# First-level steps of a row of LSTM levels are placed between the steps of the second level's chains (Trainium2, one core)

## The chip, the cores and the metric

The kernel runs on one core of one Trainium2 chip. The metric is the device time in microseconds (us). Before the change it was 3021.64 us, the median of 3 runs (3020.8 to 3025.89).

## What is computed

Four graph layers follow one another, each behind a layer norm and a ReLU and with a residual sum; x is 8 batches x 2048 nodes x 128 features in float32. The change touches the end of the third layer only. It applies LSTMs over windows of nodes, for p = 1 to 4, each level on the result of the one before:

```
for p in range(1, MAX_SKIP + 1):
    nw = Tv // p
    wins = h[:, :nw * p, :].reshape(Bv * nw, p, Hd)
    last = _lstm_last(Wih[p - 1], Whh[p - 1], bih[p - 1], bhh[p - 1], wins)
    idx = jnp.arange(nw) * p + (p - 1)
    h = h.at[:, idx, :].set(last.reshape(Bv, nw, Hd))
```

One step of an LSTM is `g = x_t @ Wih.T + h @ Whh.T + bias`, four gates i, f, g, o from it, `c = sigmoid(f) * c + sigmoid(i) * tanh(g)` and `h = sigmoid(o) * tanh(c)`, from zero states. Level 1 is a window of one node, so it changes every node by itself. Level 2 is a chain of two steps (nodes 2m and 2m+1) and replaces the second node, level 3 a chain of three steps, level 4 one of four.

## The kernel before

The program is a row of stages; the recurrence, function `recurrences` (L1861), comes before the last graph product and the perceptron. It handles two batches (k = 0, 1) at once, a pair, and four pairs one after another. The features lie on the 128 partitions and the 2048 nodes on the columns, sorted by their residue modulo 4, so that each residue is a block of 512 columns.

**The steps.** `lstm_units` (L1829) lists 18 steps: 0 to 3 are level 1, one for each residue; 4 and 5 a chain of level 2 (residues 0 and 1), 6 and 7 the other (residues 2 and 3); 8 to 10 and 11 to 13 the two chains of level 3; 14 to 17 the chain of level 4. A `Unit` has its level p, its place q in the chain, its columns, and `source`, the last earlier step whose result it reads as input. A step with q = 0 has no hidden part and no forget gate: 3 gates. The others have 4 gates and two parts. Every engine walks through this list, for each step k = 0 and then k = 1.

**TensorE**, `gates_of` (L2215): float32 values are split into a high and a low part, so a gate is 3 matmuls (L2239, or L2244 for columns in descending pieces) for the input part and 3 more (L2253) for the hidden part. Before the input part it waits for the low part of its source (`low`) and for the gates of the step before to have been read out of PSUM (`activated`, L2234), since each batch has one set of four banks. Before the hidden part it waits for the low part of the step before (L2250).

**ScalarE**, `evaluate` (L2049): one activation for each gate (L2058). The first waits until the cell update of the step before is done, the output gate until the output of the step before is done, since the gate tile is single. `squash` (L2064) is the tanh of the cell (L2067).

**VectorE**: `update` (L2132) computes the cell: one operation (L2139) for q = 0, three (L2144, L2146, L2148) otherwise. The cell tile has two halves, half 0 for the cell and half 1 for the product of input gate and candidate. `output` (L2150) is three operations (L2163, L2164, L2168): high part, value and low part of h. In the last step of a chain they go to the `hx` tiles, otherwise to the small `st` tiles, which hold one state per batch.

**The order within a step**, `turns` (L1949): if `free(n)` (q = 0, and the source older than step n - 1), the cell activation and the output of each batch are put off behind the next batch's first gates. In the other steps they stand right behind their own update:

```
yield 0, ((n - 1, 1) if n and free(n) else None), free(n)
yield 1, ((n, 0) if free(n) else None), n + 1 < NU and free(n + 1)
```

**Work beside it.** The layer norm of the pair before is woven in: on VectorE its statistics in eight parts behind steps 0 to 7 (`MEASURE`, L1925, L146), with an aggregation behind 3 and 7; POOL then takes a power (L170); on ScalarE the normalisation in parts behind steps 5 to 8 and 12 to 15 (`NORMALISE`, L182). ScalarE splits the next pair's input behind steps 9 and 16 (`SPLIT`), and POOL subtracts for its low part (L2017). In the first pair the weights of levels 2 to 4 are split ahead of steps 1, 2 and 3 (`BEHIND`, L2129). SP's queue loads and stores whole batches, and its order does not depend on the list.

## Time and profile before

| | us |
|---|---|
| median of 3 runs | 3021.64 |
| profiled execution | 3023.62 |
| its span, first to last instruction | 3021.8 |
| TensorE busy with matmuls | 2755.8 (91%) |
| VectorE busy | 1660.1 (55%) |
| ScalarE busy | 1325.6 (44%) |
| POOL busy | 172.3 (6%) |

A row of a timeline gives the start from the start of the span, the duration, the engine, the line of the kernel and the tiles; several instructions alike may be merged (x3). In brackets stands the idle time of that engine before it and what released it; where an instruction waits for several semaphores, the one that came last by the profile is named. A matmul starts before the one before it has drained, so the distance of two starts is what it takes of TensorE. PE is TensorE, DVE VectorE, ACT ScalarE, POOL GpSimd.

### The profile page before, as it was taken

Reading aid. Unit: us, or ns where it says so; the run is one execution under the profiler, and the core shown is the slowest. Engines: PE = TensorE matmul, PEld = TensorE weight load, DVE = VectorE, ACT = ScalarE, POOL = GpSimd, SP = SyncE. Lnnn points to the kernel's source line nnn. Section 1 sums busy time; section 2 is a strip of 40 time slices with the busy share of each in tenths; the row PEclk is TensorE's granted clock in tenths of the full one; section 3 lists DMA queues with packets and bytes.
Section 4 is the critical chain, followed back from the end, with each engine's and each line's share of the span. In section 5 each row is a group of like instructions: output and inputs, shape, how many; then the busy total and the mean of one; then the engine's idle time right before and its main releaser. Section 6 shows DMA issues by size and latency. Waiting matters only on the chain. (4 is left out here: it accounts for less than half of the span.)

```text
span 3021.8 us, 38552 instructions
## 1 busy us (share of the span) xinstructions
PE 2755.8 (91%) x14565; PEld 2325.4 (77%) x14565; DVE 1660.1 (55%) x3206; ACT 1325.6 (44%) x2161; POOL 172.3 (6%) x98
## 2 busy tenths in 40 slices
PE   7799998899999969999999997898989869999977
PEld 7578887899999958888877875777777757778743
DVE  7766764677777643213322124888887864332246
ACT  2765554566666532112211113666767763221135
POOL 2000102000001000000000000001010000000000
PEclk9999997999999979999999999999999989999998
DMA  8544544322223153124321223111212135331258
GB/s 349 185 150 165 179 164 149 97 61 85 71 70 98 43 177 112 56 64 145 113 70 57 66 67 108 43 43 29 84 28 56 28 84 194 98 94 56 77 205 297
DMA packets 241840, 325.88 MB, mean 108 GB/s; under 512 B 13792, under 2 KB 155136, under 8 KB 237440
## 3 DMA queue, kind: packets, MB, share of 16 engines
q1 hardware_dynamic: 238208, 310.99, 31.8%
q10 hardware_dynamic: 3456, 12.58, 1.0%
q8 instruction: 105, 1.72, 0.2%
q14 instruction: 71, 0.58, 0.1%
HBM read 226.91 MB, written 96.62 MB: 107 GB/s over the span
## 5 line engine op out<-in xcount | busy, mean ns | idle before, releaser
L993 PE MATMUL l_acc<-l_a_hi,l_g_hi 128*128 128x512 f32 x1536 | 602.6, 392 | 35.1 <-DVE l_g_lo L921 29.0
L993 PE MATMUL l_acc<-l_a_lo,l_g_hi 128*128 128x512 f32 x1536 | 599.4, 390 | 0.0
L993 PE MATMUL l_acc<-l_a_hi,l_g_lo 128*128 128x512 f32 x1536 | 599.2, 390 | 0.0
L913 DVE TENSOR_TENSOR l_a_lo<-l_raw,l_a_hi 128x512 fp32r<-128x512 f32 x192 | 132.7, 691 | 754.1 <-ACT l_a_hi L863 754.1
L1449 PE MATMUL n_acc<-n_hb,n_p 128*128 128x129 f32 x4096 | 472.3, 276 | 25.1 <-DVE n_p L1365 19.9
L863 ACT ACTIVATE l_a_hi<-l_raw 128x512 fp32r<-128x512 f32 x192 | 121.1, 631 | 846.5 <-PE l_acc L993 818.2
L1449 PEld LDWEIGHTS n_acc<-n_hb,n_p 128*128 128x128 f32 x4096 | 464.3, 192 | 29.2 <-issue 15.6
L993 PEld LDWEIGHTS l_acc<-l_a_hi,l_g_hi 128*128 128x128 f32 x1536 | 289.5, 188 | 97.0 <-DVE l_g_lo L921 29.2
L1365 DVE SCALAR_TENSOR_TENSOR n_p<-n_e,n_cols,c_mT 128x2048 f32<-128x2048 f32 x128 | 296.7, 2345 | 89.7 <-ACT n_e L1326 71.0
L2058 ACT ACTIVATE r_gate<-r_ps,r_bias 128x512 f32<-128x512 f32 (+2 forms) x504 | 298.0, 639 | 103.4 <-PE r_ps L2253 77.8
L993 PEld LDWEIGHTS l_acc<-l_a_lo,l_g_hi 128*128 128x128 f32 x1536 | 289.5, 188 | 61.3 <-issue 1.4
L993 PEld LDWEIGHTS l_acc<-l_a_hi,l_g_lo 128*128 128x128 f32 x1536 | 289.4, 188 | 60.4
L1326 ACT ACTIVATE n_e<-n_row,n_cols 128x2048 f32<-128x2048 f32 x128 | 261.7, 2088 | 13.4 <-DVE n_p L1365 11.0
L676 PE MATMUL l_acc<-l_a_hi,l_g_hi 128*128 128x512 f32 x512 | 201.1, 393 | 22.3 <-DVE l_a_lo L581 18.5
L676 PE MATMUL l_acc<-l_a_lo,l_g_hi 128*128 128x512 f32 x512 | 199.9, 390 | 0.0
L676 PE MATMUL l_acc<-l_a_hi,l_g_lo 128*128 128x512 f32 x512 | 199.9, 390 | 0.0
L2239 PE MATMUL r_ps<-r_hx_hi,r_w_hi 128*128 128x512 f32 (+2 forms) x376 | 141.8, 377 | 18.2 <-ACT r_gate L2058 13.5
L2239 PE MATMUL r_ps<-r_hx_lo,r_w_hi 128*128 128x512 f32 (+2 forms) x376 | 139.1, 370 | 0.0
L2239 PE MATMUL r_ps<-r_hx_hi,r_w_lo 128*128 128x512 f32 (+2 forms) x376 | 138.9, 369 | 0.0
L2253 PE MATMUL r_ps<-r_st_hi,r_w_hi 128*128 128x512 f32 (+2 forms) x288 | 110.1, 382 | 25.4 <-DVE r_st_lo L2168 25.4
L676 PEld LDWEIGHTS l_acc<-l_a_hi,l_g_hi 128*128 128x128 f32 x512 | 96.6, 189 | 45.5 <-DVE l_g_lo L597 18.2
L460 ACT ACTIVATE l_raw<-l_raw 128x512 f32<-128x512 f32 x128 | 79.5, 622 | 94.2 <-DMA l_raw<-in_adjT_dram 94.0
(263 smaller groups left out, 3797.0 us busy)
## 6 DMA issues: line engine op xcount, KB each, us to landing
l_raw<-in_adjT_dram SPq DMA_DIRECT2D x256, 256.0 KB, 2.8
l_raw<-in_rows_dram SPq DMA_DIRECT2D x64, 256.0 KB, 3.0
l_hraw<-h SPq DMA_DIRECT2D x32, 512.0 KB, 3.4
z<-l_res SPq DMA_DIRECT2D x64, 256.0 KB, 2.7
m_z<-z SPq DMA_DIRECT2D x16, 1024.0 KB, 5.2
l_xt<-in_x_dram SPq DMA_DIRECT2D x30, 512.0 KB, 3.5
d_xt<-in_x_dram SPq DMA_DIRECT2D x16, 512.0 KB, 15.6
n_hb<-h SPq DMA_DIRECT2D x8, 1024.0 KB, 5.9
```

Of the source, the lines that this page charges most:

```text
L460: last = act.activation(raw[:, gp % R, k], raw[:, gp % R, k], ACT.Copy, accum_out=parts[:, k, gp % T, gp // T:gp // T + 1])
L676: last = pe.matmul(acc[:, b], lhs[:, s, b * D:(b + 1) * D], rhs[:, gp % R], start=(s == 0 and lhs is g_hi and rhs is a_hi), stop=(s == T - ...
L863: act.activation(a_hi[:, gp % RING], raw[:, gp % RING], ACT.Copy).then_inc(a_high, 1)
L913: dve.tensor_tensor(a_lo[:, gp % RING], raw[:, gp % RING], a_hi[:, gp % RING].bitcast(F32), ALU.subtract).then_inc(a_low, 1)
L993: last = pe.matmul(acc[:, b], lhs[:, s, b * D:(b + 1) * D], rhs[:, gp % RING], start=(s == 0 and lhs is g_hi and rhs is a_hi), stop=(s == ...
L1326: act.activation(e[:, j % DEPTH], row[:, b.par], ACT.Relu, bias=cols[:, b.par, 1, j:j + 1], scale=cols[:, b.par, 2, j:j + 1]).then_inc(rai ...
L1365: dve.scalar_tensor_tensor(pr[:, j % DEPTH].rearrange("p (c i) -> p c i", i=P), e[:, j % DEPTH].rearrange("p (c i) -> p c i", i=P), cols[: ...
L1449: last = pe.matmul(acc[:, k, o:o + D + 1], pr[:, j % DEPTH, t * P:(t + 1) * P], hb[:, b.par, j], start=(j == 0 and o == 0), stop=(j == T - 1),
L2058: act.activation(gate[k][:, g, 0:size], ps[k][:, g, 0:size], ACT.Tanh if g == 2 else ACT.Sigmoid, bias=bias[:, 2, units[n].p - 1, g:g + 1] ...
L2239: last = pe.matmul(halves_of(ps[k][:, g, 0:size], unit, unit.length), wg, runs_of(h[k], unit.runs, unit.length), start=(m == 0), stop=(q = ...
L2253: last = pe.matmul(ps[k][:, g, 0:size], w[:, 1, p - 1, g * D:(g + 1) * D], h[k][:, 0:size], start=False, stop=(m == 2), skip_group_check=n ...
```

## The change

The list of steps is put in another order: level 1 of residues 0 and 1, first step of the first chain of level 2, level 1 of residue 2, second step of the first chain, level 1 of residue 3, then both steps of the second chain (6 and 7). Levels 3 and 4 keep their places. The sources follow the new numbers. A level 1 step now holds its cell in half 1 of the cell tile (`cell_of`), because the cell of a chain stays in half 0 across it. `chained` gives the step whose hidden state a step reads, `raw_step` the number of a level 1 step among its like, and `RAW_READ` the step from which the pair's input tiles are free for POOL's next subtraction.

```diff
--- before.py
+++ after.py
@@ -1829,12 +1829,13 @@
 def lstm_units():
 
     block = lambda s: RESIDUE_AT[s] * 512
-    units = [Unit(1, 0, 512, [block(s)], 512, 512, -1) for s in range(SKIP)]
-    for first in (0, 2):
-        for q in range(2):
-            units.append(Unit(2, q, 512, [block(first + q)], 512, 512, first + q))
+    first_level = lambda s: Unit(1, 0, 512, [block(s)], 512, 512, -1)
+    second = lambda first, q, source: Unit(2, q, 512, [block(first + q)], 512, 512, source)
+
+    units = [first_level(0), first_level(1), second(0, 0, 0), first_level(2), second(0, 1, 1), first_level(3),
+             second(2, 0, 3), second(2, 1, 5)]
     piece = lambda m: block(m % SKIP) + THIRD_AT[m // SKIP]
-    for g, length, kept, sources in ((2, 170, 170, (5, 7, 7)), (0, 172, 171, (7, 5, 5))):
+    for g, length, kept, sources in ((2, 170, 170, (4, 7, 7)), (0, 172, 171, (7, 4, 4))):
         for q in range(3):
             units.append(Unit(3, q, 2 * length, [piece(3 * g + q), piece(3 * g + 3 + q)], length, kept,
                               sources[q]))
@@ -1918,6 +1919,7 @@
         block = ctx.enter_context(nc.Block())
         NPAIR = B // 2
         NRAW = sum(u.p == 1 for u in units)
+        RAW_READ = max(n for n, u in enumerate(units) if u.p == 1) + 1
         SPLIT = {NRAW + 5: 0, NRAW + 12: 1}
         NL = NU - 1
 
@@ -1941,6 +1943,17 @@
         def later(i):
 
             return not isinstance(i, int) or i > 0
+
+        def cell_of(k, n):
+
+            return cell[k][:, 1 if units[n].p == 1 else 0, 0:units[n].size]
+
+        def chained(n):
+
+            return max(m for m in range(n) if units[m].p == units[n].p)
+
+        def raw_step(n):
+            return sum(u.p == 1 for u in units[:n])
 
         def free(n):
 
@@ -2012,7 +2025,7 @@
             def split_next(i):
 
                 for k in pair:
-                    pool.wait_ge(summed[k], i * NG + before[NRAW])
+                    pool.wait_ge(summed[k], i * NG + before[RAW_READ])
                     pool.wait_ge(raw_high[k], i + 2)
                     pool.tensor_tensor(raw_lo[k][:, :], raw[k][:, :], raw_hi[k][:, :].bitcast(F32),
                                        ALU.subtract).then_inc(raw_split[k], 1)
@@ -2064,7 +2077,7 @@
             def squash(i, n, k):
                 size = units[n].size
                 act.wait_ge(cell_ready[k], i * NU + n + 1)
-                act.activation(tc[k][:, 0:size], cell[k][:, 0, 0:size], ACT.Tanh).then_inc(squashed[k], 1)
+                act.activation(tc[k][:, 0:size], cell_of(k, n), ACT.Tanh).then_inc(squashed[k], 1)
 
             def normalise(i, k, blocks):
                 b = i * 2 + k
@@ -2131,7 +2144,7 @@
 
             def update(i, n, k):
                 size, q = units[n].size, units[n].q
-                c, ig = cell[k][:, 0, 0:size], cell[k][:, 1, 0:size]
+                c, ig = cell_of(k, n), cell[k][:, 1, 0:size]
                 ga = lambda g: gate[k][:, g, 0:size]
                 at = i * NG + before[n]
                 dve.wait_ge(activated[k], at + 2)
@@ -2218,9 +2231,9 @@
                 first = isinstance(i, int) and i == 0
                 if first and (n == 0 or p > units[n - 1].p):
                     pe.wait_ge(w_split, 2 * p - 1)
-                if first and n < SKIP - 1:
-                    pe.wait_ge(first_split[k], n + 1)
-                elif n == (SKIP - 1 if first else 0):
+                if p == 1 and first and raw_step(n) < SKIP - 1:
+                    pe.wait_ge(first_split[k], raw_step(n) + 1)
+                elif p == 1 and raw_step(n) == (SKIP - 1 if first else 0):
                     pe.wait_ge(raw_split[k], i + 1)
                 elif p > 1:
                     pe.wait_ge(low[k], i * NL + unit.source + 1)
@@ -2247,7 +2260,7 @@
                     if q == 0:
                         last.then_inc(summed[k], 1)
                 if q:
-                    pe.wait_ge(low[k], i * NL + n)
+                    pe.wait_ge(low[k], i * NL + chained(n) + 1)
                     for g in gates[n]:
                         for m, (w, h) in enumerate(h_parts):
                             last = pe.matmul(ps[k][:, g, 0:size], w[:, 1, p - 1, g * D:(g + 1) * D],
```

## Rows read from the trace of the kernel before

**Rows 1.** The page, its first line
```profile
span 3021.8 us, 38552 instructions
```

**Rows 2.** Busy time by engine (instructions), clock, DMA: steps 0 to 7, second pair
```profile
core 0: us, PE busy (x) PEld busy (x) DVE busy (x) ACT busy (x) POOL busy (x), PEclk, DMA share, GB/s
2014.40:2073.90 59.50, 51.02 (x204) 38.85 (x205) 51.78 (x116) 43.59 (x74) 3.74 (x2) 0.97 0.13 36
```

**Rows 3.** TensorE's waits in the recurrence: us in total, times, longest
```profile
PE r_ps L2253 <- DVE r_st_lo L2168: 25.4, 17, 4.5
PE r_ps L2239 <- ACT r_gate L2058: 19.2, 20, 3.3
```

**Rows 4.** TensorE's timeline, second pair: start, us, instruction, [idle before]
```profile
2033.03 0.50 PE L2239 MATMUL r_ps<-r_hx_hi,r_w_hi 128*128 128x512 f32 x1 [0.24 <-ACT r_gate L2058]
...
2036.49 0.47 PE L2239 MATMUL r_ps<-r_hx_hi,r_w_hi 128*128 128x512 f32 x1 [1.10 <-DVE r_hx_lo L2168]
...
2039.01 0.50 PE L2239 MATMUL r_ps<-r_hx_hi,r_w_hi 128*128 128x512 f32 x1 [0.17 <-ACT r_gate L2058]
...
2046.60 0.79 PE L2253 MATMUL r_ps<-r_st_hi,r_w_hi 128*128 128x512 f32 x1 [4.54 <-DVE r_st_lo L2168]
...
2050.84 0.40 PE L2239 MATMUL r_ps<-r_hx_hi,r_w_hi 128*128 128x512 f32 x1
...
2061.22 0.50 PE L2239 MATMUL r_ps<-r_hx_hi,r_w_hi 128*128 128x512 f32 x1 [0.42 <-ACT r_gate L2058]
...
2065.46 0.50 PE L2253 MATMUL r_ps<-r_st_hi,r_w_hi 128*128 128x512 f32 x1 [1.17 <-DVE r_st_lo L2168]
...
2073.96 0.32 PE L2239 MATMUL r_ps<-r_hx_hi,r_w_hi 128*128 128x340 f32 x1
```

**Rows 5.** Busy time by engine and granted clock in three stretches
```profile
1888.30:1899.20 10.90, 7.70 (x30) 5.39 (x30) 10.48 (x18) 7.72 (x13) 0.00 (x0) 1.00 0.72 192
2033.00:2041.90 8.90, 7.60 (x30) 5.40 (x30) 8.61 (x38) 5.97 (x10) 0.51 (x1) 1.00 0.01 2
2046.60:2050.90 4.30, 4.30 (x13) 3.46 (x14) 3.24 (x8) 1.93 (x3) 0.00 (x0) 0.65 0.00 0
```

**Rows 6.** VectorE's timeline, second pair, from the end of slot 2
```profile
2032.96 0.87 DVE L146 BATCH_NORM_STATS2 rln_six<-r_xt 128x6 f32<-128x128 f32 x4
...
2033.75 0.68 DVE L2139 TENSOR_TENSOR r_cell<-r_gate 128x512 f32<-128x512 f32 x1
...
2036.34 0.68 DVE L2139 TENSOR_TENSOR r_cell<-r_gate 128x512 f32<-128x512 f32 x1
...
2041.22 0.69 DVE L2139 TENSOR_TENSOR r_cell<-r_gate 128x512 f32<-128x512 f32 x1
...
2041.82 0.71 DVE L2163 TENSOR_TENSOR r_hx_hi<-r_gate,r_tc 128x512 fp32r<-128x512 f32 x1
...
2050.29 0.69 DVE L2144 TENSOR_TENSOR r_cell<-r_gate 128x512 f32<-128x512 f32 x1 [0.96 <-ACT r_gate L2058]
...
2053.25 0.69 DVE L2163 TENSOR_TENSOR r_hx_hi<-r_gate,r_tc 128x512 fp32r<-128x512 f32 x1 [0.77 <-ACT r_tc L2067]
```

**Rows 7.** ScalarE's timeline, second pair
```profile
2035.66 1.85 ACT L2058 ACTIVATE r_gate<-r_ps,r_bias 128x512 f32<-128x512 f32 x3 [0.57 <-DVE r_hx L2164]
...
2041.94 0.63 ACT L2067 ACTIVATE r_tc<-r_cell 128x512 f32<-128x512 f32 x1 [1.83 <-DVE r_cell L2139]
...
2057.29 1.64 ACT L182 ACTIVATE r_hn<-r_xt,rln_shift,rln_scale 128x128 f32<-128x128 f32 x4
```

**Rows 8.** TensorE's timeline: step 5's hidden part, first pair
```profile
1899.23 0.67 PE L2253 MATMUL r_ps<-r_st_hi,r_w_hi 128*128 128x512 f32 x1 [2.16 <-DVE r_st_lo L2168]
```

**Rows 9.** POOL's timeline, second pair
```profile
2041.39 3.28 POOL L170 TENSOR_TENSOR rln_scale<-rln_var_eps,rln_half 128x16 f32<-128x16 f32 x1 [36.35 <-DVE rln_var_eps L159]
...
2094.82 4.62 POOL L2017 TENSOR_TENSOR r_raw_lo<-r_raw,r_raw_hi 128x2048 fp32r<-128x2048 f32 x1 [8.47 <-ACT r_raw_hi L2086]
```

**Rows 10.** VectorE's timeline at POOL's subtraction
```profile
2095.57 4.23 DVE L2144 TENSOR_TENSOR r_cell<-r_gate 128x340 f32<-128x340 f32 x1 [1.04 <-ACT r_gate L2058]
```

## The prediction

> **What bounds the kernel now.** I read the page first, then the stretches of the recurrence, then TensorE's waits there, then each engine's timeline through one pair of batches. (n,k) is step n of the unit list for batch k of the pair; a light step has 3 gates and no hidden part, a heavy one 4 gates and both parts.
>
> The span is 3021.8 us [rows 1]; the diff touches only the recurrence. In a pair's first eight steps (the four of level 1 and the four of level 2) VectorE is busy 51.8 of 59.5 us, as much as TensorE's 51.0 [rows 2]. TensorE waits 25.4 us for VectorE's low part of a hidden state and 19.2 us for ScalarE's gates over all pairs [rows 3]. The largest single wait is in step 5: its input part starts at 2039.01 and is 12 matmuls long, then the hidden part starts only at 2046.60, 4.54 us late [rows 4]. Two more follow, 0.42 at (6,0) and 1.17 at (7,0). After the 4.54 us the granted clock of that stretch is 0.65, so part of it ran at 1.2 GHz and not 2.4 [rows 5].
>
> Why 4.54: five light steps stand in a row. From 2065.46 to 2073.96 TensorE runs 36 matmuls (the hidden part of one batch, 12, and the whole step of the other, 24) [rows 4]: 0.235 us each, so 2.8 us for a part of a heavy step, 5.6 for a heavy step of one batch, 2.1 for a light one and 4.2 for a light one of both batches. VectorE needs for a light step 2 x (0.6 update + 2.0 output), as from 2033.75 to 2036.34, and 0.8 of layer-norm statistics (2032.96 to 2033.75), 6.0 us [rows 6]. So it falls behind by 1.8 us a step, and the fourth statistics part with its aggregation costs 2.3 (2033.75 to 2041.22 is 7.47, less 5.2) [rows 6]. Step 5 needs the state of step 4, the newest thing VectorE has.
>
> **The change, part by part.**
>
> *Instructions.* None is added or removed; the same matmuls, activations, vector operations and DMAs are issued. No DMA is moved: SP's order is the same. POOL's split waits for step 5's sums instead of step 3's, and then, as now, for ScalarE's copy that follows step 9; cost nothing, covered by those four steps. The other half of the cell tile costs nothing: same shape, same engines. Weight splits stay behind steps 0 to 2, and level 2's are finished before (2,0); nothing.
>
> *Removed.* The chain 0-1 of level 2 becomes steps 2 and 4 with a light step between. (4,0) starts its input part at 2033.03 as step 4 does now (same gate condition), ends it 2.8 us later at 2035.9, and needs the state of (2,0), which VectorE finishes before its slot 3 begins at 2033.75 [rows 6]. So the 4.54 goes, and the slow clock behind it: 12 matmuls took 4.24 us (2046.60 to 2050.84) [rows 4] and not 2.80, 1.44 us.
>
> *What is late next.* I carry the second pair's clock times on. Step 3 now ends with the output of (3,1), which is put off today, so VectorE's slot 3 is 2.0 longer, and with 2.3 of statistics ends at 2043.2. The update of (4,0), 2.0 us for a heavy one (its activation can follow at 2052.5, as 2053.25 less 0.77 tells) [rows 6], ends at 2045.3. ScalarE's cell activation of (4,0) must wait for it (0.63 us, as the one at 2041.94) [rows 7], and because step 4 is heavy it is not put off: the four gates of (4,1) stand behind it on ScalarE. They have been summed since 2044.5 but are read from 2045.9 to 2048.3 (0.58 apart) [rows 7]. TensorE runs (4,0) and (4,1) through to 2044.3, (5,0) to 2046.4, and (5,1) must wait for these gates until 2048.4: a new wait of 1.7 us. VectorE then has the output of (4,0) to 2048.1, the update of (4,1) to 2050.1, 0.78 of statistics; ScalarE's last gate of (5,0) comes at 2051.5, that of (5,1) at 2053.7. So (6,0) waits 0.8 and starts 2051.5, (6,1) 0.2 and starts 2053.8. A normalisation part of 1.6 us (the four at 2057.29) [rows 7] and the output of (5,0) put the last gate of (6,0) at 2057.5: (7,0) waits 1.5. Its input part ends at 2060.4, and the state of (6,0), third in VectorE's row behind the output of (5,1) and the update of (6,1), is there at 2062.2: 1.7 more. From 2062.3 TensorE has 2.8 + 5.6 us without a wait: step 8 starts at 2070.7. Today it starts at 2073.96 [rows 4]. **Gain 3.3 us a pair.** Check by waits: today 4.54 + 0.42 + 1.17, 1.10 at (4,1), 0.2 at (5,0), and 1.44 of clock, 8.9 together; after, 1.7 + 0.8 + 0.2 + 1.5 + 1.7 = 5.9. That gives 3.0, near enough.
>
> The first pair has no statistics, but weight splits in their place; its wait in step 5 is 2.16 [rows 8] with matmuls of 0.67 us behind it, and by the same steps its gain comes out at 3.5. I take 3.3 x 4 = 13.2 us. From step 8 on the order is the old one, and both VectorE (its heavy update of step 7 ends at 2072.4 and now at about 2075.5) and TensorE enter it about 3.3 earlier, so the gain is kept.
>
> *The clock.* New waits of 1.5 to 1.7 are not shown today. The wait of 1.10 at 2036.49 [rows 4] left the clock at 1.00; the 2.16 of the first pair [rows 8], behind 10.9 us with TensorE busy 7.70 [rows 5], did not. A fall at (7,0) would reach the end whole, 1.44 a pair; bounds 0 and 1.44, and twice that if (5,1) falls too. 1.6 lies midway between the two observed cases, so I charge half of 1.44, 2.9 us in all. 13.2 - 2.9 = **10.3 us saved**.
>
> The profiled execution took 3023.62 (its span and 1.8 around it), so the sum gives 3013.3 for it. The median of the runs shown is 3021.64, 2.0 lower; from that, **3011.3 us**.
>
> **POOL beside the heavy update.** The power operation of the layer norm starts as the statistics end, 3.28 us long at 2041.39; now it would start at 2043.3, beside the heavy update of (4,0). Beside it today VectorE's operations with two SBUF inputs kept 0.69 to 0.71 [rows 6]. But beside POOL's 4.62 us subtraction at 2094.82 [rows 9] VectorE's heavy update operation took 4.23 us for 340 columns, where 512 take 0.69 [rows 10]. I charge 0, since the same short POOL operation stands beside the same kind of vector operation; the bound is 3.3 a pair.
> By the Trainium skill (SBUF — State Buffer, two separate sides) a vector operation with two SBUF inputs and a POOL operation that reads SBUF share one port pair by an exclusive lock held for the whole instruction, and the loser blocks. The trace agrees for the long subtraction and not for the 128x16 power. Taken at its word the rule would block the update for 3.28 us, in three pairs; it is the slower rival below.
>
> **Rivals.**
> *The clock gives it back.* It falls both at (5,1) and at (7,0) in every pair: 4 x 2 x 1.44 = 11.5 of 13.2, saving 1.7: **3020**. For it: the waits come closer together, and 2.16 was enough once. Against: at (5,1) ScalarE and VectorE, not TensorE, set the pace, so most of that fall is hidden. 0.17.
> *POOL stops the heavy update (slower).* If the power blocks VectorE for 3.3 us at (4,0), all that I derived behind 2043 moves by 3.3 in three pairs, 9.9 us; the wait at (5,1) becomes 5.0, more than today's 4.54, so the clock surely falls there and probably at (7,0): 4 x 2 x 1.44 = 11.5. 13.2 - 9.9 - 11.5 = 8.2 slower: **3030**. It decides from 3.3 us of delay a pair. Against it: the 0.69 to 0.71 beside the power now. 0.08.
> *More than my table.* The clock never falls and the input-side gaps close: at most VectorE's idle time in the stretch, 59.5 - 51.8 = 7.7 a pair [rows 2], of which the start and each heavy step's wait for its own activation (0.77 before 2053.25) [rows 6] stay. I put it at 5.0 a pair: **3001.6**. 0.07.
> *The forecast*, 7 to 17 us saved: 0.66. The rest, 0.02, is left over.
>
> **The numbers.** Range: below 3003 lies most of the last rival, above 3021 the slower one and a piece of the clock's. A measurement of this kernel can tell about 0.2%, 6 us. Faster by more than 6: the forecast, the last rival, nothing of the others: 0.73. Within: the clock's rival and a sliver: 0.18. Slower: 0.09.
>
> **What would show it.** TensorE's wait for the low state falls from 25.4 to about 13 us (the first chain's gone, 2.16 in the first pair [rows 8] and 4.54 in the second, with the other two taken like it 15.8 in all; the second chain's grown by 0.5 to 1.2 a pair), and its wait for gates grows from 19.2 to about 30, with a new 1.7 at (5,1). From the first matmul of a pair to step 8: 56.2 us instead of 59.5. The update of (4,0) keeps 0.69 a piece beside POOL's power. The granted clock stays above 0.8 in any 4 us of the stretch in about half of the pairs. I am wrong if a wait of over 4 us stands at (5,1) or (7,0), if VectorE's heavy update beside the power takes 3 us, or if step 8 comes less than 1.5 us or more than 5 us earlier.

## The result, and the profile after

The changed kernel took 3010.09 us (median of 7 runs, 3005.25 to 3017.99), the kernel before it 3022.22 on the same chip (7 runs, 3020.8 to 3029.3): ratio 0.9956, 95% interval 0.9946 to 0.9967. 3011.3 had been forecast. The profiled execution took 3011.66 us, 1.8 of it around its span; the profiled one of before took 3023.62, so the two traces that are compared here lie 11.96 us apart.

The page's first line, beside [rows 1] (the number of instructions is the same):

```profile
span 3009.9 us, 38552 instructions
```

Busy time by engine, granted clock and DMA of the changed kernel. The first row is the recurrence, from the first matmul of the first pair to the start of the last row of transposes (shown below), the second row all that follows, the third and fourth are steps 0 to 7 of the second and the third pair (columns as in [rows 2]):

```profile
1863.20:2453.40 590.20, 529.44 (x2584) 442.58 (x2584) 482.57 (x935) 419.41 (x764) 49.23 (x18) 0.98 0.18 51
2453.40:3009.90 556.50, 487.36 (x1937) 353.30 (x1937) 214.26 (x371) 163.54 (x231) 7.87 (x7) 0.95 0.45 146
...
2012.30:2068.40 56.10, 49.70 (x204) 37.84 (x205) 51.31 (x116) 42.52 (x74) 3.93 (x2) 1.00 0.14 38
2161.30:2217.50 56.20, 50.05 (x206) 38.10 (x205) 51.32 (x115) 42.70 (x74) 3.79 (x2) 0.99 0.13 38
```

The same two stretches of before:

```profile
1862.60:2467.40 604.80, 537.75 (x2585) 448.33 (x2585) 484.14 (x935) 423.43 (x763) 49.13 (x18) 0.96 0.17 50
2467.40:3021.80 554.40, 488.02 (x1937) 354.93 (x1937) 214.19 (x371) 163.34 (x231) 7.88 (x7) 0.95 0.44 147
```

The last row of transposes in the changed kernel, where its first stretch ends:

```profile
2453.43 1.94 PE L2281 MATMUL r_ps<-k_ident,r_hx 128*128 128x128 f32 x16 [1.33 <-DVE r_hx L2177]
```

The recurrence is 14.6 us shorter (604.80 less 590.20), more than the whole span gained. What follows it, which the change does not touch, took about 2 us more, and the recurrence began 0.6 later. TensorE's busy time in the recurrence is 8.3 us less for the same matmuls, and its granted clock 0.98 instead of 0.96: its idle time there falls by 6.3 (from 67.1 to 60.8). So nearly half of the gain is waits and the rest is clock. For the second pair [rows 2] has 59.50 us at 0.97, the row above 56.10 at 1.00.

The time of each stage, taken as the difference of two starts in TensorE's timeline (first matmul of a pair, first of step 8, first row of transposes behind step 17):

| pair | steps 0 to 7, before | after | saved | steps 8 to 17, before | after |
|---|---|---|---|---|---|
| first | 62.91 | 59.54 | 3.37 | 83.06 | 83.66 |
| second | 59.47 | 56.05 | 3.42 | 88.17 | 85.92 |
| third | 59.36 | 56.17 | 3.19 | 88.04 | 87.82 |
| fourth | 59.57 | 55.88 | 3.69 | 80.32 | 80.34 |

13.67 us are saved in steps 0 to 7, much the same in each pair, and none is given back in steps 8 to 17. These 13.67 are what the change brings. The other 0.9 of the recurrence's 14.6 is the clock at places that the change does not touch: in steps 8 to 17 of the second pair it fell before and not after (2.25 saved), and at the turn from the second to the third pair it fell after and not before (0.9 lost).

TensorE's waits in the recurrence, beside [rows 3] (us in total, times, longest):

```profile
PE r_ps L2252 <- ACT r_gate L2071: 28.9, 24, 3.2
PE r_ps L2266 <- DVE r_st_lo L2181: 13.7, 12, 1.8
```

TensorE's timeline, second pair, beside [rows 4]; the last row is the first pair's hidden part of (7,0), the longest such wait there, where [rows 8] had 2.16 in step 5:

```profile
2033.81 0.39 PE L2266 MATMUL r_ps<-r_st_hi,r_w_hi 128*128 128x512 f32 x1
...
2046.15 0.50 PE L2252 MATMUL r_ps<-r_raw_hi,r_w_hi 128*128 128x512 f32 x1 [1.69 <-ACT r_gate L2071]
...
2049.21 0.50 PE L2252 MATMUL r_ps<-r_hx_hi,r_w_hi 128*128 128x512 f32 x1 [0.70 <-ACT r_gate L2071]
...
2055.23 0.50 PE L2252 MATMUL r_ps<-r_hx_hi,r_w_hi 128*128 128x512 f32 x1 [1.34 <-ACT r_gate L2071]
...
2059.92 0.50 PE L2266 MATMUL r_ps<-r_st_hi,r_w_hi 128*128 128x512 f32 x1 [1.63 <-DVE r_st_lo L2181]
...
2068.42 0.32 PE L2252 MATMUL r_ps<-r_hx_hi,r_w_hi 128*128 128x340 f32 x1
...
1914.23 0.50 PE L2266 MATMUL r_ps<-r_st_hi,r_w_hi 128*128 128x512 f32 x1 [1.80 <-DVE r_st_lo L2181]
```

The hidden part of (4,0) starts at 2033.81 behind its input part with no bracket: the 4.54 us are gone. In their place stand 1.69 at (5,1), 0.70 at (6,0), 1.34 at (7,0) and 1.63 at its hidden part.

VectorE's timeline at the heavy update of (4,0):

```profile
2038.21 0.69 DVE L2181 TENSOR_TENSOR r_hx_lo<-r_hx,r_hx_hi 128x512 fp32r<-128x512 f32 x1
2038.82 0.87 DVE L146 BATCH_NORM_STATS2 rln_six<-r_xt 128x6 f32<-128x128 f32 x4
...
2041.09 0.68 DVE L2157 TENSOR_TENSOR r_cell<-r_gate 128x512 f32<-128x512 f32 x1
2041.69 0.71 DVE L2159 TENSOR_TENSOR r_cell<-r_gate,r_cell 128x512 f32<-128x512 f32 x1
2042.43 0.69 DVE L2161 TENSOR_TENSOR r_cell<-r_cell 128x512 f32<-128x512 f32 x1
```

ScalarE's, behind it:

```profile
2043.16 0.63 ACT L2080 ACTIVATE r_tc<-r_cell 128x512 f32<-128x512 f32 x1 [5.28 <-DVE r_cell L2161]
2043.70 3.56 ACT L2071 ACTIVATE r_gate<-r_ps,r_bias 128x512 f32<-128x512 f32 x6
```

POOL's, in the same time:

```profile
2041.26 3.27 POOL L170 TENSOR_TENSOR rln_scale<-rln_var_eps,rln_half 128x16 f32<-128x16 f32 x1 [38.36 <-DVE rln_var_eps L159]
```

ScalarE stands 5.28 us for the cell of (4,0) and only then reads the sums of (4,1), as the forecast had it. POOL's power overlaps all three operations of the heavy update (the first for most of its length), and they keep 0.68 to 0.71 us.

### The profile page after: what moved, and what is told of

It is laid out like the page before. It is cut to its first block and busy times, and to the rows that moved or that the text cites. A ratio compares the mean times of both kernels' runs of the same rounds, so it can differ in the third digit from the quotient of the medians.

```text
span 3009.9 us, 38552 instructions
## 1 busy us (share of the span) xinstructions
PE 2746.2 (91%) x14565; PEld 2318.1 (77%) x14565; DVE 1658.9 (55%) x3206; ACT 1321.1 (44%) x2161; POOL 172.3 (6%) x98
## 5 line engine op out<-in xcount | busy, mean ns | idle before, releaser
L2080 ACT ACTIVATE r_tc<-r_cell 128x512 f32<-128x512 f32 (+2 forms) x144 | 84.9, 590 | 91.0 <-DVE r_cell L2161 81.6
```

What stands on the lines that cost most here:

```text
L2080: act.activation(tc[k][:, 0:size], cell_of(k, n), ACT.Tanh).then_inc(squashed[k], 1)
```

## The experiments

Each was timed in five rounds beside the kernel before. Since what follows the recurrence scatters (below), the recurrence itself is given too: the first matmul of the first pair to the start of the last row of transposes, in the one profiled execution; before 604.8, after 590.2.

**1. Is it the separation of the two steps, or the number of light steps ahead?** The chain of level 2 earlier, but its two steps side by side:

```diff
-    units = [first_level(0), first_level(1), second(0, 0, 0), first_level(2), second(0, 1, 1), first_level(3),
-             second(2, 0, 3), second(2, 1, 5)]
+    units = [first_level(0), first_level(1), second(0, 0, 0), second(0, 1, 1), first_level(2), first_level(3),
+             second(2, 0, 4), second(2, 1, 5)]
```

> The changed kernel with another order of the list: level 1 of residues 0 and 1, then both steps of the first chain side by side, then level 1 of residues 2 and 3, then the second chain. No step stands between the steps of a chain, but only three light steps stand ahead of the first heavy one. Theory 1 (VectorE's backlog: it needs 6.0 us for a light step where TensorE needs 4.2, so what counts is how many light steps stand in a row ahead of a heavy one): the wait of the first chain's hidden part falls from 4.5 to about 2.5 us in pairs 2 to 4, the first eight steps take about 56.9 us (before 59.5, changed 56.1), 8 to 11 us saved against before; up to 1.4 a pair less if the clock falls. Rival (distance: what counts is a step between producer and reader): the 4.5 us wait stays, within 3 us of before.

Measured: 3021.14 us (12 runs), before 3024.81 (20 runs), ratio 0.9986 (0.9975 to 0.9997); recurrence 600.8. TensorE's timeline, second pair:

```profile
2034.70 0.50 PE L2266 MATMUL r_ps<-r_st_hi,r_w_hi 128*128 128x512 f32 x1 [2.71 <-DVE r_st_lo L2181]
...
2065.91 0.50 PE L2266 MATMUL r_ps<-r_st_hi,r_w_hi 128*128 128x512 f32 x1 [1.81 <-DVE r_st_lo L2181]
```

Only three light steps stand ahead of the chain's second step here, where before there were five, and its hidden part waits 2.71 us, near what theory 1 had; the clock fell behind it and behind the 1.81. The third pair, where it fell once less, took 58.16 us for steps 0 to 7, the second 59.87. So the time did not follow: 3.7 us saved and not 8 to 11. Most of the gain needs the light step between the two. (The sum that run 4 leads to gives 3.1 us for this wait, with an ordinary part of the statistics, 0.8 us, in the gap and not the fourth one with its 2.3.)

**2. The light step between them, with one more light step ahead:**

```diff
-    units = [first_level(0), first_level(1), second(0, 0, 0), first_level(2), second(0, 1, 1), first_level(3),
-             second(2, 0, 3), second(2, 1, 5)]
+    units = [first_level(0), first_level(1), first_level(2), second(0, 0, 0), first_level(3), second(0, 1, 1),
+             second(2, 0, 2), second(2, 1, 4)]
```

(and the sources of level 3 follow: 5 where 4 stood.)

> The changed kernel with the list: level 1 of residues 0, 1 and 2, first step of the first chain, level 1 of residue 3, second step of the first chain, then the second chain. Five light steps stand in a row as before, but one of them between the two steps of the chain. Theory 1 in its plain form (only the number of light steps ahead counts) would leave the hidden part of the first chain late. Theory 2 (both: the backlog makes the newest state late, the distance decides whether the reader needs the newest): no wait at the first chain's hidden part, a wait of about 2 us for gates at the first batch after it, and VectorE's queue paces the rest, so the first eight steps take the same 56 to 57 us as the changed kernel, within 3 us of it in all.

Measured: 3012.30 us (6 runs), ratio 0.9962 (0.9946 to 0.9977); recurrence 590.8. No wait stands ahead of the first chain's hidden part; the two longest in the second pair, with a fall of the clock behind the first:

```profile
2051.31 0.47 PE L2252 MATMUL r_ps<-r_hx_hi,r_w_hi 128*128 128x512 f32 x1 [1.82 <-ACT r_gate L2071]
...
2059.36 0.50 PE L2266 MATMUL r_ps<-r_st_hi,r_w_hi 128*128 128x512 f32 x1 [1.21 <-DVE r_st_lo L2181]
```

Here five light steps in a row stand ahead of the chain's second step, as before, and the whole gain is there. So one step of distance inside the chain is enough, whatever the number of light steps ahead.

**3. The wait that took its place at (5,1).** The changed kernel, with the output of a chain's second step put off again wherever its forerunner is not the step just before:

```diff
-            return units[n].q == 0 and units[n].source < n - 1
+            return (units[n].q == 0 or chained(n) < n - 1) and units[n].source < n - 1
```

> The changed kernel, but a heavy step whose chain predecessor is older than the step before (step 4) also puts its cell activation and output off. By the hand schedule the new wait of 1.7 us at (5,1) comes from ScalarE standing at the cell activation of (4,0): then it goes, (6,0)'s 0.7 too, VectorE has no gap in slot 4, and the state of (6,0) comes 0.9 us earlier: the wait at (7,0)'s hidden part grows to about 3 us and step 8 starts 0.9 a pair earlier, 3 to 4 us less than the changed kernel if the clock holds, 2 us more if it falls behind the 3 us wait. Rival (the wait is for the matmuls' sums or for VectorE's queue alone): the waits stay and the time too.

Measured: 3006.43 us (6 runs, 3003.25 to 3015.13), ratio 0.9945 (0.993 to 0.996); recurrence 593.8 in its profiled execution, which was one of its two longest (3014.84). The wait at (5,1) is gone, but (6,1) now waits 1.09, and the hidden part of (7,0) waits longer (1.82, where I had expected about 3), with a fall of the clock behind it in each of pairs 2 to 4, in the second four matmuls later:

```profile
2062.75 0.50 PE L2266 MATMUL r_ps<-r_st_hi,r_w_hi 128*128 128x512 f32 x1 [1.82 <-DVE r_st_lo L2181]
...
2063.79 0.58 PE L2266 MATMUL r_ps<-r_st_lo,r_w_hi 128*128 128x512 f32 x1
2064.16 0.63 PE L2266 MATMUL r_ps<-r_st_hi,r_w_lo 128*128 128x512 f32 x1
```

Steps 0 to 7 took 57.01, 56.83 and 56.67 us in these pairs, 0.7 to 1.0 more than in the changed kernel, although the median was lower. Run 11 takes that up.

**4. Is the wait of 4.54 a backlog that VectorE builds up step by step?** The kernel before, with three of the four parts of the statistics left out (the aggregation reads the last part's for all blocks, at the old place):

```diff
+        if part and hi < self.blocks:
+            return
         for b in range(lo, hi):
...
-        if hi < self.blocks:
-            return
...
-            last = dve.bn_aggr(self.mv[:, b], self.six[:, b])
+            last = dve.bn_aggr(self.mv[:, b], self.six[:, lo + b % (hi - lo)])
```

> The kernel before, with 12 of the 16 layer-norm statistics of each batch left out (the aggregation reads the last four again), so that VectorE has 0.78 us less in three of the light steps ahead of step 5, in pairs 2 to 4; the matmuls are the same. Backlog theory: the 4.5 us wait falls to about 2.2 us in these pairs and the first eight steps to 55 to 56 us, 9 to 14 us saved in all; it shows too whether a wait of 2.2 us brings the slow clock. Rival (the wait is the latency of step 4's own chain of gates, cell, output): it stays at 4.5 and less than 3 us are saved.

Measured: 3013.42 us (7 runs), ratio 0.9966 (0.9955 to 0.9977); recurrence 596.9.

```profile
2042.16 0.79 PE L2253 MATMUL r_ps<-r_st_hi,r_w_hi 128*128 128x512 f32 x1 [4.53 <-DVE r_st_lo L2168]
```

The wait is 4.53 us, as before. From the second pair's start to the end of that wait it is 30.23 us and was 32.11: that stretch became 1.9 us shorter, of the 2.3 that VectorE no longer does, and the wait did not move. The backlog that my prediction named is not what makes it. The rival, which had the wait right, had the time wrong (under 3 us saved, 11.4 measured): steps 0 to 7 of the four pairs saved 3.6, and 4.5 more came in steps 8 to 17 of pairs 2 and 3, where the clock did not fall behind the first wait in this execution. That the edit brought this part is not shown.

*What does.* TensorE's start of step 5 is itself paced by VectorE. (5,0) began at 2039.01 behind a gate of (4,0) [rows 4], and ScalarE's output gate of that step stands behind VectorE's r_hx: the output of (3,0), which VectorE has written, two operations behind the update of (3,1) at 2036.34 [rows 6], at 2038.2. ScalarE's row of that gate, then VectorE's next operation and the one that ends the wait, in the kernel before:

```profile
2038.27 1.84 ACT L2058 ACTIVATE r_gate<-r_ps,r_bias 128x512 f32<-128x512 f32 x3 [0.24 <-DVE r_hx L2164]
...
2038.34 0.69 DVE L2168 TENSOR_TENSOR r_hx_lo<-r_hx,r_hx_hi 128x512 fp32r<-128x512 f32 x1
...
2045.86 0.69 DVE L2168 TENSOR_TENSOR r_st_lo<-r_st,r_st_hi 128x512 fp32r<-128x512 f32 x1
```

VectorE has no idle time between the two. So a delay ahead of it moves both ends of the wait alike. The wait is what VectorE does from there to the state of (4,0), which ends at 2046.5: the low part of (3,0), the fourth part of the statistics with the aggregation, the update of (4,0), the output of (3,1), the update of (4,1), the output of (4,0): 0.6 + 2.3 + 0.6 + 2.0 + 0.6 + 2.0 = 8.1 us, less 0.7 for a gate and 2.8 for 12 matmuls: 4.6. Of that only 2.3 are statistics, and only those that stand in that gap. Without them 2.3 should be left, and the first pair, which has none, had 2.16 [rows 8]. The expectations below call this theory 3.

**5. The changed kernel again**, with no edit, beside runs 6 to 8:

> The changed kernel itself, beside the others on one chip. Both theories: 10 to 16 us under the kernel before. In the profile: the same waits of about 1.7, 0.7, 1.3 and 1.6 us at (5,1), (6,0), (7,0) and (7,0)'s hidden part; whether the clock falls behind the 1.7 or 1.6 in another execution is open.

Measured: 3010.58 us (5 runs), before 3025.27 (13 runs), ratio 0.9953 (0.994 to 0.9966); recurrence 590.9, waits 1.69, 0.69, 1.34 and 1.64, no fall of the clock in steps 0 to 7 of pairs 2 to 4. The first result repeats: steps 0 to 7 saved 14.0 us, steps 8 to 17 next to nothing.

**6. Theory 3 tested in the old order.** The kernel before, with the statistics from the fourth part on one step later, out of the gap:

```diff
-        MEASURE = {n: (n // 4, PARTS[n % 4]) for n in range(8)}
+        MEASURE = {n + (n > 2): (n // 4, PARTS[n % 4]) for n in range(8)}
...
-                        if not stream and n == 4:
+                        if not stream and n == 5:
```

> The kernel before, in its old order, with the fourth statistics part and the aggregation (2.3 us of VectorE) moved from behind step 3 to behind step 4, and the four of the second batch one step later. New theory, since leaving out earlier statistics left the wait at 4.5: TensorE's start of step 5 is itself paced by VectorE (through the output gate of step 4, which waits for the output of step 3), so the wait is what VectorE has between the output of (3,0) and that of (4,0), less one gate and 12 matmuls: with 2.3 us less there it is 2.2 in pairs 2 to 4, as in the first pair, and 5 to 7 us are saved. Rival (backlog: VectorE's total up to step 5): it falls by no more than VectorE's total does ahead of it, which is the same 2.3, so both give 2.2 here; what tells them apart is the run with fewer statistics. A third (nothing is saved, because VectorE's total up to step 7 is the same): within 2 us of before.

Measured: 3013.73 us (5 runs), ratio 0.9966 (0.9953 to 0.9979); recurrence 593.0. TensorE's timeline, second and third pair:

```profile
2042.94 0.50 PE L2253 MATMUL r_ps<-r_st_hi,r_w_hi 128*128 128x512 f32 x1 [2.22 <-DVE r_st_lo L2168]
...
2192.73 0.50 PE L2253 MATMUL r_ps<-r_st_hi,r_w_hi 128*128 128x512 f32 x1 [2.15 <-DVE r_st_lo L2168]
```

The wait falls by 2.3 us, to what theory 3 gives. With no step moved at all, the old order then does steps 0 to 7 in 57.65, 55.73 and 55.73 us: the third and fourth pair as fast as the changed kernel's. The second pair's extra 1.9 us is the clock, which fell behind 2.22 and not behind 2.15:

```profile
2012.80:2070.50 57.70, 51.63 (x206) 39.19 (x205) 50.81 (x111) 43.61 (x74) 3.93 (x2) 0.96 0.13 37
2163.00:2218.80 55.80, 49.73 (x205) 37.87 (x206) 50.60 (x111) 43.46 (x74) 3.79 (x2) 1.00 0.13 38
```

**7. The price of the clock.** The kernel before, with nine matmuls of zeros ahead of the first chain's hidden part in step 5:

```diff
+                if p == 2 and q and n == 5 and k == 0:
...
+                    for _ in range(9):
+                        pe.matmul(ps[k][:, gates[n][0], 0:size], w_hi[:, 1, p - 1, 0:D], fill[:, 0:size],
+                                  start=False, stop=False, skip_group_check=True)
                 if q:
```

> The kernel before, with 9 more matmuls of a zero tile into the same sums ahead of the hidden part of (5,0), 2.1 us of work inside the wait of 4.5 (2.16 in the first pair). Nothing else changes. Theory: the clock no longer falls behind that wait, 12 matmuls take 2.8 us instead of 4.2, 1.4 us a pair and about 5 to 6 in all are saved; so that much of the change's gain was the clock's. Rival (VectorE or ScalarE paces that stretch too, or the clock falls anyway): within 2 us of before.

Measured: 3019.58 us (7 runs), ratio 0.9979 (0.9968 to 0.9989); recurrence 601.2.

```profile
2044.41 0.79 PE L2265 MATMUL r_ps<-r_st_hi,r_w_hi 128*128 128x512 f32 x1 [2.43 <-DVE r_st_lo L2174]
...
2198.02 0.50 PE L2265 MATMUL r_ps<-r_st_hi,r_w_hi 128*128 128x512 f32 x1 [2.35 <-DVE r_st_lo L2174]
```

Nine matmuls (2.1 us) left 2.43 of the wait, and the clock still fell in the second and fourth pair (59.49 and 59.57 us), but not in the third (58.03). That is the price of one fall: 1.5 us. Even there the stage stays 2 us above the changed kernel's, so the wait itself is the larger part.

**8. Statistics out of the bottleneck in the changed kernel.** The second batch's statistics and normalisation in steps 8 to 11:

```diff
-        MEASURE = {n: (n // 4, PARTS[n % 4]) for n in range(8)}
+        MEASURE = {n + 4 * (n // 4): (n // 4, PARTS[n % 4]) for n in range(8)}
...
-                        if not stream and n == 4:
+                        if not stream and n == 8:
```

> The changed kernel with the second batch's statistics moved from behind steps 4 to 7 to behind steps 8 to 11, where TensorE waits little for VectorE. Theory (VectorE's queue between the outputs paces steps 5 to 7 of the changed kernel): the wait at (7,0)'s hidden part shrinks from 1.6 towards 0.5, the first eight steps take 54 to 55 us in pairs 2 to 4 instead of 56.1, and steps 8 to 17 give back under 1 us: 3 to 5 us less than the changed kernel. Rival (ScalarE paces them): the time stays.

Measured: 3014.35 us (6 runs), ratio 0.9966 (0.9954 to 0.9978); recurrence 594.9. A miss, about 4 us longer than the changed kernel's on the same chip (3010.58 and 590.9), with intervals that overlap. Steps 0 to 7 became only 0.5 us shorter (55.61, 55.44, 55.44): the hidden wait at (7,0) went from 1.63 to 1.17, while 1.34 at its input part, which is for ScalarE, stayed. The statistics then met a bottleneck in steps 8 to 17:

```profile
2111.61 0.66 PE L2266 MATMUL r_ps<-r_st_hi,r_w_hi 128*128 128x344 f32 x1 [3.93 <-DVE r_st_lo L2181]
```

TensorE's wait for the low state rose to 21.8 us in total, and steps 8 to 17 took 88.3, 90.3 and 82.2 us.

**9. Run 3's order with its fall of the clock filled.** The same insertion as in run 7, six matmuls, at `n == 7 and k == 0`:

> The kernel of e3_put_off_heavy (the changed kernel with the heavy update of step 4's cells put off as in the old order) with six more matmuls of zeros, 512 columns each, ahead of the hidden part of the first chain of step 7: 1.4 us of work of no use in the place of a wait of 1.82 us, behind which the clock of TensorE fell in three pairs. Theory A (the clock, not the wait, is what that order loses): the wait shrinks to about 0.4 us, no matmul of 0.8 us stands in steps 0 to 7 of pairs 2 to 4, these steps take 55.4 us instead of 56.7 to 57.0, and the time falls by 4 to 6 us below that of e3 (3001 to 3003). Theory B (the clock falls whatever stands there, or the added matmuls reach past the wait, since VectorE sets the pace): steps 0 to 7 stay at 56.7 or grow, and the time is that of e3 within 2 us.

Measured: 3009.66 us (6 runs), before 3023.72 (14 runs), ratio 0.9958 (0.9943 to 0.9972); recurrence 589.9. Busy time and clock of steps 0 to 7, then of steps 8 to 17, second pair:

```profile
2010.90:2066.20 55.30, 50.93 (x211) 39.08 (x212) 51.27 (x115) 43.06 (x74) 3.87 (x2) 1.00 0.14 39
2066.20:2154.00 87.80, 81.22 (x415) 71.66 (x413) 67.27 (x129) 61.75 (x120) 12.76 (x4) 0.94 0.24 68
```

As theory A had it inside the stage: 1.4 us of useless matmuls, 0.41 of the wait left, no fall, and 55.2 and 55.1 us in pairs 2 and 3 (the fourth had 56.12, with a fall of the clock in step 0, right behind the turn). The time did not follow: 3009.66, not 3001 to 3003, and 0.8 under run 3's own kernel on the same chip (3010.45, run 11). Part stands in the second row, 87.8 us at a clock of 0.94, which other executions did in 85.9.

**10. Run 3's order with run 6's edit:**

```diff
-        MEASURE = {n: (n // 4, PARTS[n % 4]) for n in range(8)}
+        MEASURE = {n + (n > 2): (n // 4, PARTS[n % 4]) for n in range(8)}
```

> The kernel of e3_put_off_heavy with the fourth part of the first batch's statistics and its aggregation one step later (from behind step 3 to behind step 4), and the second batch's parts one step later too, so that its last part falls behind step 8. Theory 3 (TensorE waits for what VectorE does between two outputs, and 2.3 us of that is the fourth part with its aggregation; VectorE has no gap from 2033 to 2064 us in e3): moving it by one step stays inside that stretch and shrinks none of the later waits (0.49, 1.09, 1.35 and 1.82 us, sum 4.75) by more than 0.5 us in sum, but the second batch's last part with its aggregation, 2.3 us too, leaves the stretch ahead of the hidden part of (7,0) only where it stood there; it stood behind it, so steps 0 to 7 stay at 56.7 to 57.0 us and the time at e3's within 2 us. Rival (the place of the aggregation is what costs, as in the old order, where moving it took 2.3 us from one wait): the waits of steps 5 to 7 fall by 2 us in sum, the clock stays at full speed there, steps 0 to 7 take 54 to 55 us, and the time is 3000 or less.

Measured: 3012.81 us (9 runs), ratio 0.9964 (0.9952 to 0.9976); recurrence 593.7; steps 0 to 7 56.77, 56.84 and 56.73 us, as expected.

```profile
2050.83 0.77 PE L2252 MATMUL r_ps<-r_hx_hi,r_w_hi 128*128 128x512 f32 x1 [2.52 <-DVE r_hx_lo L2181]
```

The sizes were right and the path was not: I had the waits of steps 5 to 7 nearly unmoved, but the aggregation now stands ahead of an output that (6,1) needs, and its wait grew from 1.09 to 2.52 with the fall of the clock behind it, while the one at (7,0) shrank to 1.17. What helps in one order (run 6) is neutral in another.

**11. Run 3 again**, with no edit:

> The kernel of e3_put_off_heavy again, beside the two built on it. If its order is truly faster than the changed kernel's, as the median of its six runs says (3006.4 beside 3010.1 to 3010.6), the median comes out at 3004 to 3009 with the wait of 1.82 us and the clock fall behind it in each pair; if that median was the luck of few executions (its steps 0 to 7 took 0.6 to 1 us more than the changed kernel's in its profile), it comes out at 3010 to 3014.

Measured: 3010.45 us (6 runs, 3006.56 to 3013.3), ratio 0.9955 (0.9942 to 0.9969); recurrence 589.6. So most of run 3's lead was the luck of few executions; that its order is as fast as the changed kernel's or a little faster is open. Steps 0 to 7, second and third pair, of one execution of one kernel:

```profile
2012.70:2069.50 56.80, 51.05 (x205) 38.96 (x206) 51.42 (x115) 43.11 (x74) 3.87 (x2) 0.97 0.13 38
2161.50:2216.60 55.10, 49.41 (x205) 37.86 (x206) 51.09 (x115) 43.20 (x74) 3.80 (x2) 1.00 0.14 38
```

And the wait ahead of each's last hidden part:

```profile
2059.45 0.50 PE L2266 MATMUL r_ps<-r_st_hi,r_w_hi 128*128 128x512 f32 x1 [1.81 <-DVE r_st_lo L2181]
...
2208.09 0.50 PE L2266 MATMUL r_ps<-r_st_hi,r_w_hi 128*128 128x512 f32 x1 [1.80 <-DVE r_st_lo L2181]
```

The same wait brought 1.2 GHz in the second pair and not in the third, and that is 1.7 us. Where it did not, steps 0 to 7 are 0.8 to 1.1 us shorter than the changed kernel's, as the expectation of run 3 had it for a clock that holds.

**12. All three places filled.** Run 9, with matmuls of zeros in steps 8 and 9 too:

```diff
+                        if (n, k) == (8, 1) and g == gates[n][-1] and m == 2:
+                            for _ in range(8):
+                                pe.matmul(ps[k][:, g, 0:size], w_hi[:, 1, p - 1, 0:D], fill[:, 0:size],
+                                          start=False, stop=False, skip_group_check=True)
...
+                idle = 6 if (n, k) == (7, 0) else 4 if (n, k) == (9, 0) else 0
```

> The kernel of e9_put_off_filler with matmuls of zeros in two more places of each pair: eight of 340 columns (1.25 us) ahead of the last matmul of the second chain's step 8, where TensorE then waited 1.38 us, and four of 340 columns (0.6 us) ahead of the hidden part of the first chain's step 9. Behind that wait the clock fell in pair 2 of e9 for 6.4 us (pair 3 of the changed kernel, pairs 2 and 3 of the kernel before), and these pairs took 87.9 us in steps 8 to 17 where the others took 85.8. Theory A (short waits in a row bring the clock down there, and where they do differs between executions): with work in their place no stretch of low clock of over 5 us stands in steps 8 to 10 of pairs 2 and 3, steps 8 to 17 take 85.8 to 86.3 in both, and the median is 3005 to 3008. Theory B (the clock falls there for another reason, or the matmuls of zeros delay the gates behind them): the stretch stays in one pair or more, or steps 8 to 17 take 87 or more without it, and the median is 3009 or more.

Measured: 3008.92 us (5 runs, 3008.22 to 3012.52), before 3026.14 (9 runs), ratio 0.9943 (0.993 to 0.9957); recurrence 587.6, the shortest of all.

```profile
1863.90:2451.60 587.70, 540.78 (x2657) 453.21 (x2657) 482.61 (x935) 421.73 (x764) 48.92 (x18) 0.98 0.18 52
2070.20:2156.20 86.00, 80.09 (x428) 70.22 (x427) 67.28 (x129) 61.83 (x120) 12.49 (x4) 0.98 0.24 70
```

In pairs 2 and 3 no stretch of low clock of over 5 us is left behind step 8, and steps 8 to 17 took 85.93 and 85.82 us in pairs 2 and 3, which speaks for theory A; the median, 3008.9, lies between what A and B gave. The recurrence is 2.6 us shorter than the changed kernel's in its profile (587.6 and 590.2), with more matmuls; but run 3's kernel alone differs by 4.2 between two executions (593.8 and 589.6). And 0.9943 and 0.9956 have intervals that overlap: no version was shown to beat the changed kernel's time.

## Why the prediction was right, and where it was not

*The hand-carried table* held. The changed kernel's second pair begins 2.12 us earlier (its first matmul at 2012.37 and not 2014.49), so each time of the prediction is to be read with 2.12 less: update of (4,0) from 2041.1 (measured 2041.09); (5,1) from 2046.3 (2046.15); (6,0) from 2049.4 (2049.21); the hidden part of (7,0) from 2060.2 (2059.92); step 8 at 2068.6 (2068.42). The four waits forecast as 1.7, 0.8, 1.5 and 1.7 were 1.69, 0.70, 1.34 and 1.63. The fifth, 0.2 at (6,1), was not there. Steps 0 to 7: 56.2 forecast, 56.05 measured; the wait for the low state about 13, measured 13.7; for gates about 30, measured 28.9.

*The first pair* gained 3.37 us, where 3.5 came out of the same steps. *Steps 8 to 17* kept the gain, as argued; the 2.25 that the second pair gained there besides is the clock, and run 5 does not have it.

*The sum* of 13.2 was right (13.67 in steps 0 to 7, 14.0 in run 5; 14.6 and 14.0 over the recurrence). **The term that failed is the clock's: "I charge half of 1.44, 2.9 us in all".** Nothing was lost there: the granted clock is 1.00 and 0.99 in the rows above, and in both profiled executions of this kernel it did not fall in steps 0 to 7 of pairs 2 to 4. The size of one fall was right (1.5, 1.7 and 1.9 us in runs 7, 11 and 6 against 1.44); what was off is how often. Waits of 1.60 to 1.69 brought no fall in any pair of these two executions, while 1.79 to 1.82 did in 8 of 14 cases over all traces. Half of the pairs was too dear for a wait of 1.6, and would have been fair for one of 1.8. The step behind it failed too: it put the chance midway between a wait of 1.10 and one of 2.16, as if the length decided. The kernel before already shows otherwise. In step 8 of its second pair the clock fell behind a wait of 1.39 (at 2080.3), and in the fourth pair it did not:

```profile
2078.31 0.46 PE L2244 MATMUL r_ps<-r_hx_hi,r_w_hi 128*128 128x170 f32 x2 [1.39 <-ACT r_gate L2058]
...
2388.18 0.46 PE L2244 MATMUL r_ps<-r_hx_hi,r_w_hi 128*128 128x170 f32 x2 [1.39 <-ACT r_gate L2058]
```

That the forecast of 3011.3 met 3010.1 in spite of the term is luck in part: with no charge for the clock it would have been 3008.4, and in the profiled execution the stages that the change does not touch took 1.7 us more in sum (0.9 less in the recurrence, 2.0 more behind it, 0.6 more ahead of it). The profiled pair differ by 11.96, the medians of seven runs by 12.1, and the ratio's interval allows 10 to 16 us.

*The reason given for the 4.54 us fell*, though its number was right: "it falls behind by 1.8 a step". Run 4 took the statistics of the earlier steps away and left the wait whole; run 6 took only the fourth part out of the gap and left 2.22. The forecast did not suffer, because the table carried each engine's work by the clock and never used the 1.8. With the right reason I would have seen that the change has a cheaper twin: the fourth part one step later does most of it in the old order (3013.73 against 3010.58 on the same chip; in steps 0 to 7 of pairs 2 to 4 it saves 9.3 us, the changed kernel 10.3).

*The clock gives it back* (3020): it did not. *POOL stops the heavy update* (3030): the power lay over all three operations and they kept 0.68 to 0.71 us, so the row beside the short power, and not the one beside the 4.62 us subtraction [rows 9, 10], was the one to go by. By the Trainium skill (SBUF — State Buffer, two separate sides) the update should have been blocked for the whole of POOL's instruction; this trace does not agree for the 128x16 power. *More than my table* (3001.6): this kernel did not; run 12, the nearest to it, saved 17 us in the recurrence (604.8 less 587.7), yet its median is 3008.9.

*Why behind the same wait the clock falls in one pair and not in the next*, no run was made to test, but the kept traces show what goes with it. In each of the fourteen, all changes of the granted clock within the recurrence (some 200 in all) lie on one even raster, to 0.002 us, that runs on through the four pairs, whatever the kernel does. Of the fourteen waits of 1.79 to 1.82, the eight that began 0.1 to 1.3 us behind a point of it brought a fall, and the six that began 1.8 us or more behind one did not. Of the waits of 1.37 to 1.39 in step 8, the 11 that began from 0.1 before such a point to 0.6 behind it did, and the 24 others did not. The Trainium skill (TensorE: Matmul & The Clock Gate, Part 1) says that the clock follows an activity count which runs free of the kernel, so that it changes at different points from one time to the next; these traces agree with that. By this, one thing above may be luck: none of the twelve waits of 1.60 to 1.69 in steps 5 and 7 of the changed kernel's two traces (pairs 2 to 4) began in that last stretch, so that such a wait keeps the clock wherever it lies is not shown.

What stays open: that the changed order is better than run 3's, or run 12 than the changed one, is not shown either.

## What to carry to other kernels

When two engines wait for each other in a ring, a wait is not the sum of what came before it but the work between the two events that bracket it; before moving steps, find both brackets and see whether one item in the gap (here 2.3 us of statistics) can simply stand elsewhere. To price a reordering, carry every engine's clock through one period by hand: that gave four waits to within 0.2 us. Judge small edits by the stage they touch, since the rest of the program scatters by more than they bring, and within that stage count the falls of the clock before you call a difference the edit's.

## What the hardware showed that was not expected

The part behind the recurrence, whose instructions no run changed, took 553.2 to 560.3 us in the fourteen profiled executions (from the start of the last row of transposes to the end of the span): a scatter of 7 us against a change worth 12. It is one reason why runs 3, 9, 11 and 12, which differ by up to 6 us in the recurrence of their profiled executions (593.8, 589.9, 589.6, 587.6), differ by 4, in another order, in their medians (3006.4, 3009.7, 3010.5, 3008.9).

A second source lies in the recurrence itself. In steps 8 and 9 the clock falls in some pairs and not in others, in the same kernel, behind the same wait of 1.37 to 1.39 us. In the changed kernel, third pair:

```profile
2221.86 0.46 PE L2257 MATMUL r_ps<-r_hx_hi,r_w_hi 128*128 128x170 f32 x2 [1.37 <-ACT r_gate L2071]
...
2223.53 0.63 PE L2257 MATMUL r_ps<-r_hx_lo,r_w_hi 128*128 128x170 f32 x2
```

And second pair, where the rows behind it stay at 0.39:

```profile
2072.77 0.46 PE L2257 MATMUL r_ps<-r_hx_hi,r_w_hi 128*128 128x170 f32 x2 [1.37 <-ACT r_gate L2071]
2073.07 0.39 PE L2257 MATMUL r_ps<-r_hx_lo,r_w_hi 128*128 128x170 f32 x2
```

Steps 8 to 17 took 87.82 and 85.92 us in these two. Matmuls of zeros in the place of that wait (run 12) left no such fall in the one profiled execution.
